# Gated two-layer block, its FP4 MLP on one core: VectorE's roundings, GpSimd's unscalings and the last two pairs in another order

## The reference

```
x = x + tanh(g_xattn[0]) * attention(layernorm(x), ctx, ctx)
x = x + tanh(g_ffn[0])   * experts(layernorm(x))
x = x + tanh(g_xattn[1]) * autocorrelation(layernorm(x), ctx, ctx)
x = x + tanh(g_ffn[1])   * mlp(layernorm(x))
```

```
def fp4_quant_dequant(x):
    scale = max(|x|, over the block) / 6, at least 1e-12
    xn = x / scale
    q = nearest of (0, .5, 1, 1.5, 2, 3, 4, 6) to |xn|, with xn's sign, times scale
gate = fp4_linear(x, w_gate);  y = fp4_linear(x, w_up)      # 128 -> 352
h = silu(gate) * y
return fp4_linear(h, w_down)                                 # 352 -> 128
```

## Time and profile before

| What | Value |
|---|---|
| median of 3 runs | 276.76 us (275.24 to 281.72) |
| span of the profiled execution | 274.8 us |
| own time of the profiled execution | not listed apart from the three runs; the lowest of them is 0.4 us above the span |
| TensorE busy | 253.9 us, 92% |
| VectorE busy | 190.7 us, 69% |
| ScalarE busy | 164.6 us, 60% |
| GpSimd busy | 131.0 us, 48% |
| first hh of the MLP starts | 221.16 us |
| last copy on ScalarE starts | 272.58 us |

### The profile page before, as it was taken

The page is one execution under the profiler, slowest core; times in us unless marked ns, Lnnn a source line. Parts: engine busy times, 40 slices in busy tenths (PEclk is TensorE's granted clock), DMA queues, the critical chain, the costliest instruction groups (busy, mean ns, idle before and its releaser), DMA issues.

```text
span 274.8 us, 6251 instructions
## 1 busy us (share of the span) xinstructions
PE 253.9 (92%) x2152; PEld 196.4 (71%) x2152; DVE 190.7 (69%) x494; ACT 164.6 (60%) x384; POOL 131.0 (48%) x207
## 2 busy tenths in 40 slices
PE   8999999999899989999999999979998784989886
PEld 6655376666577868999999999665785442766675
DVE  3898688888988763253222223885769989999993
ACT  2369985666488654675566667473445793354453
POOL 4566579999402403218992220275066633353230
PEclk9999999999999998999999999999999999799999
DMA  6999000000000209776777771000000000000111
GB/s 191 379 348 403 13 4 2 2 4 0 2 2 4 76 20 377 300 289 265 296 300 291 292 290 63 2 1 1 4 0 0 0 0 2 0 19 23 38 39 38
DMA packets 12191, 30.11 MB, mean 110 GB/s; under 512 B 1024, under 2 KB 5248, under 8 KB 12032
## 3 DMA queue, kind: packets, MB, share of 16 engines
q1 hardware_dynamic: 12160, 29.71, 28.5%
HBM read 9.71 MB, written 1.05 MB: 39 GB/s over the span
## 4 chain that ended last, share of the span: by engine, by line
PE 64%; DVE 20%; issue 7%; ACT 5%; POOL 2%; DVEq 0%; POOLq 0%
PE ps L1403 12%; PE ps L1414 12%; PE ps L1252 6%; DVE s_region L294 4%; PE ps L1226 4%; PE ps L1239 4%; PE ps L1159 3%; DVE s_region L1090 3%; PE ps L1542 3%; PE ps L1150 2%; DVE s_small L1095 2%; PE ps L1262 2%; PE ps L1151 2%; PE ps L1344 2%; DVE s_small L237 2%
## 5 line engine op out<-in xcount | busy, mean ns | idle before, releaser
L631 ACT ACTIVATE s_region<-ps,s_region 128x128 f32<-128x128 f32 x144 | 40.8, 371 | 21.8 <-PE ps L1403 21.8
L960 DVE SCALAR_TENSOR_TENSOR s_ctxT<-ps,s_region,s_ctxT 128x64 f32 x72 | 18.1, 281 | 43.8 <-PE ps L1414 43.8
L1403 PE MATMUL ps<-s_region 128*128 128x128 f32 x288 | 38.0, 276 | 0.3 <-issue 0.3
L1414 PE MATMUL ps<-s_region 128*128 128x128 f32 x288 | 37.9, 275 | 0.0
L1403 PEld LDWEIGHTS ps<-s_region 128*128 128x128 f32 x288 | 34.9, 192 | 0.7 <-issue 0.7
L1414 PEld LDWEIGHTS ps<-s_region 128*128 128x128 f32 x288 | 35.0, 192 | 0.2 <-issue 0.2
L420 POOL COPY s_region<-s_xt 128x64 f32 x72 | 14.8, 234 | 32.3 <-PE ps L1403 24.5
L574 ACT COPY s_region<-ps 128x512 f32<-128x512 f32 x32 | 17.2, 592 | 16.2 <-PE ps L1239 16.2
L830 DVE TENSOR_REDUCE s_small<-ps 128x16 f32<-128x1024 f32 x16 | 19.6, 1224 | 9.7 <-PE ps L1226 9.7
L1599 PE MATMUL ps<-s_region 128*128 128x352 f32 x64 | 21.1, 469 | 5.3 <-DVE s_region L1090 3.7
L301 POOL TENSOR_TENSOR s_region<-s_region,s_small 128x704 f32<-128x704 f32 (+2 forms) x11 | 14.6, 1330 | 22.0 <-DVE s_region L294 21.7
(11 more groups left out here) (230 smaller groups left out, 528.7 us busy)
## 6 DMA issues: line engine op xcount, KB each, us to landing
s_region<-s_wall SPq DMA_DIRECT2D x36, 514.0 KB, 3.0
...
```

What stands on the lines that cost most here:

```text
L631: ins = act.activation(hg[j % 3][:, c, :], ps[:, j % 3, RPT * S * c:RPT * S * (c + 1)], ACT.Gelu, bias=wbuf[j % 6][:, FF + FC * D + c:FF + ...
L960: dve.scalar_tensor_tensor(row, ps[:, 4 + j % 2, S * k:S * k + S], w, row, ALU.mult, ALU.add).then_inc(m["acc_done"], 1)
L1403: ins = mm(ps[:, j % 3, RPT * S * c:RPT * S * (c + 1)], w[:, P * c:P * c + P], xg[j % 4], start=True, stop=True)
L1414: ins = mm(ps[:, 4 + j % 2, 0:RPT * S], w[:, FF + D * c:FF + D * c + D], hg[j % 3][:, c, :], start=(c == 0), stop=(c == FC - 1))
```

## The change

It has five parts, all in the MLP.

- VectorE: in pairs 1 and 3 the roundings of x stand behind the shrink of h, directly ahead of the roundings of h. Ahead of pair 0, `x_scale` and `sum_stats` are split, so that the statistics of group 3 stand between the reciprocal and the shrink of x group 1.
- GpSimd: in q = 1 and 3 it unscales h first and x after it. The small scale operations are gone.
- ScalarE: its copies of turned x and turned h are now activations with the function Copy and the constant scale `FINE / 6` (`unscaled_copy`).
- `WHOLE` is 7: pair 6 is rounded whole, by `h_round(6)` right behind hh of pair 7, and unscaled by GpSimd. Pair 7 alone goes by halves; its shrink is done in halves too, and each half's magnitude waits for its own half.
- TensorE: in q = 3 and 5 the gate product stands ahead of the down products; the turn of an x group stands ahead of `down`, in q = 2 and 4 instead of behind the gate in q = 1 and 3. Before the gate of pair 3 there is a wait for the roundings of x group 2 (`xd_done`). Behind the loop come the turn of pair 6, the residuals of the two halves, the down products of pair 6, both half turns, and the two half products.

SyncE sends seven pairs and two halves instead of six and four.

The diff, without the lists of names and buffers:

```diff
@@ -30,7 +30,7 @@
...
-WHOLE = PAIRS - 2
+WHOLE = PAIRS - 1
...
@@ -285,9 +285,9 @@
...
-        def fp4_scale(eng, amax, sc):
-            return eng.tensor_scalar(sc, amax, FINE / 6.0, None, ALU.mult)
+        def unscaled_copy(act, out, src):
+            return act.activation(out, src, ACT.Copy, scale=FINE / 6.0)
         def fp4_off(eng, out, mag, z):
@@ -466,11 +466,8 @@
...
             def x_unscale(g):
-                pool.wait_ge(m["xv_done"], g + 1)
-                fp4_scale(pool, xmx[g % 2], xsc[g % 2]).then_inc(m["xsc_ready"], 1)
...
-                pool.wait_ge(m["xsc_ready"], g + 1)
-                fp4_unscale(pool, qd[g % 2], xsc[g % 2], 4 * D // BLK, qv[g % 2]).then_inc(m["xq_done"], 1)
+                fp4_unscale(pool, qd[g % 2], xmx[g % 2], 4 * D // BLK, qv[g % 2]).then_inc(m["xq_done"], 1)
...
@@ -485,25 +482,14 @@
...
-            def h_scale(q):
-                pool.wait_ge(m["hv_done"], q + 1)
-                if q >= 3:
-                    pool.wait_ge(m["hq_done"], q - 2)
-                fp4_scale(pool, hmx[q % 3], hsc[q % 3]).then_inc(m["hsc_ready"], 1)
             for q in range(1, WHOLE + 1):
...
+                pool.wait_ge(m["hd_done"], q)
+                if q >= 3:
+                    pool.wait_ge(m["ht_done"], q - 2)
+                fp4_unscale(pool, hd[u], hmx[(q - 1) % 3], 2 * NH, hq[u].rearrange("p a n -> p (a n)")).then_inc(m["hq_done"], 1)
...
-                h_scale(q - 1)
-                pool.wait_ge(m["hd_done"], q)
-                pool.wait_ge(m["hsc_ready"], q)
-                if q >= 3:
-                    pool.wait_ge(m["ht_done"], q - 2)
-                fp4_unscale(pool, hd[u], hsc[(q - 1) % 3], 2 * NH, hq[u].rearrange("p a n -> p (a n)")).then_inc(m["hq_done"], 1)
-            for q in range(WHOLE, PAIRS):
-                h_scale(q)
...
@@ -713,7 +699,7 @@
...
-                act.copy(xqT[g % 2], ps[:, 0, :]).then_inc(m["xqt_used"], 1)
+                unscaled_copy(act, xqT[g % 2], ps[:, 0, :]).then_inc(m["xqt_used"], 1)
             def silu(q):
...
@@ -721,10 +707,10 @@
...
             def magnitude(q):
-                act.wait_ge(m["hv_done"], q + 1)
                 if q >= 2:
...
-                for rows in [slice(0, 2 * NH)] if q < PAIRS - 1 else [slice(0, NH), slice(NH, 2 * NH)]:
+                for n, rows in enumerate([slice(0, 2 * NH)] if q < WHOLE else [slice(0, NH), slice(NH, 2 * NH)]):
+                    act.wait_ge(m["hv_done"], q + 1 + n)
...
             def x_magnitude(g):
@@ -757,7 +743,11 @@
             def half_turned(n):
...
-                act.copy(hT[p % 2][:, t].rearrange("p k b -> p (k b)"), ps[:, 5 + t, 0:MT * P]).then_inc(m["ht_used"], 1)
+                unscaled_copy(act, hT[p % 2][:, t].rearrange("p k b -> p (k b)"), ps[:, 5 + t, 0:MT * P]).then_inc(m["ht_used"], 1)
+            def pair_turned(q):
+                act.wait_ge(m["ht_done"], q + 1)
+                unscaled_copy(act, hT[q % 2].rearrange("p a k b -> p a (k b)"), ps[:, 5:7, 0:MT * P]).then_inc(m["ht_used"], 1)
             def half_finish(n):
...
@@ -768,23 +758,20 @@
...
                 if q >= 3:
...
+                if q >= 2:
+                    pair_turned(q - 2)
...
-                if q >= 2:
-                    act.wait_ge(m["ht_done"], q - 1)
-                    act.copy(hT[q % 2].rearrange("p a k b -> p a (k b)"), ps[:, 5:7, 0:MT * P]).then_inc(m["ht_used"], 1)
...
+            finish(WHOLE - 2)
+            pair_turned(WHOLE - 1)
+            half_turned(0)
...
-            half_turned(0)
...
-            half_turned(2)
...
-            half_turned(3)
-            half_finish(2)
-            half_finish(3)
...
@@ -1059,55 +1046,73 @@
...
+            def sum_spread(g):
...
+            def x_blocks(g):
+                nblk = 4 * D // BLK
+                return xb[:, nblk * g:nblk * (g + 1), :]
             def x_scale(g):
-                u = g % 2
...
-                    dve.wait_ge(m["xsc_ready"], g - 1)
...
-                nblk = 4 * D // BLK
-                src = xb[:, nblk * g:nblk * (g + 1), :]
-                fp4_inverse(dve, dd, src, xmx[u], xin[u])
-                fp4_shrunk(dve, blocks(qv[u]), src[:, :, 0:BLK], spread(xin[u], nblk)).then_inc(m["xv_done"], 1)
+                fp4_inverse(dve, dd, x_blocks(g), xmx[g % 2], xin[g % 2])
+            def x_shrink(g):
+                fp4_shrunk(dve, blocks(qv[g % 2]), x_blocks(g)[:, :, 0:BLK], spread(xin[g % 2], 4 * D // BLK)).then_inc(m["xv_done"], 1)
             def x_round(g):
...
+            def h_round(q):
+                u = q % 2
+                dve.wait_ge(m["hm_done"], q + 1)
+                if q >= 2:
+                    dve.wait_ge(m["hq_done"], q - 1)
+                dd.step(fp4_off(dve, blocks(hd[u]), blocks(hm[u]), hh[u]))
+                fp4_off(dve, hd[u], hm[u], hd[u]).then_inc(m["hd_done"], 1)
             def pair_step(q):
-                u, w, n3 = q % 2, (q - 1) % 2, q % 3
-                if q < PAIRS:
-                    dve.wait_ge(m["sg_done"], q + 1)
-                    dve.wait_ge(m["gu_done"], q + 1)
-                    rows = "p a (n k) -> p a n k"
-                    dve.tensor_tensor(hh[u].rearrange("p (a n) k -> p a n k", a=2), sg[u].rearrange(rows, k=BLK),
-                                      ps[:, 3:5, 0:MLP].rearrange(rows, k=BLK), ALU.mult).then_inc(m["hh_done"], 1)
-                    if q >= 3:
-                        dve.wait_ge(m["hq_done"], q - 2)
-                    dve.wait_ge(m["hh_done"], q + 1)
-                    k = dd.mark(dve.tensor_reduce(hmx[n3], hb[u], AX, ALU.max, apply_absolute_value=True))
-                    if q in (1, 3):
-                        x_round((q + 3) // 2)
-                    if q == 2:
-                        x_scale(3)
-                    dd.after(k)
-                    dd.step(dve.reciprocal(hin[n3], hmx[n3]))
+                u, n3 = q % 2, q % 3
+                dve.wait_ge(m["sg_done"], q + 1)
+                dve.wait_ge(m["gu_done"], q + 1)
+                rows = "p a (n k) -> p a n k"
+                dve.tensor_tensor(hh[u].rearrange("p (a n) k -> p a n k", a=2), sg[u].rearrange(rows, k=BLK),
+                                  ps[:, 3:5, 0:MLP].rearrange(rows, k=BLK), ALU.mult).then_inc(m["hh_done"], 1)
+                if q == WHOLE:
+                    h_round(q - 1)
+                if q >= 3:
+                    dve.wait_ge(m["hq_done"], q - 2)
+                dve.wait_ge(m["hh_done"], q + 1)
+                k = dd.mark(dve.tensor_reduce(hmx[n3], hb[u], AX, ALU.max, apply_absolute_value=True))
+                if q == 2:
+                    x_scale(3)
+                    x_shrink(3)
+                dd.after(k)
+                dd.step(dve.reciprocal(hin[n3], hmx[n3]))
+                if q < WHOLE:
...
-                    if q == 0:
-                        x_scale(2)
-                if 1 <= q <= WHOLE:
-                    dve.wait_ge(m["hm_done"], q)
-                    if q >= 3:
-                        dve.wait_ge(m["hq_done"], q - 2)
-                    dd.step(fp4_off(dve, blocks(hd[w]), blocks(hm[w]), hh[w]))
-                    fp4_off(dve, hd[w], hm[w], hd[w]).then_inc(m["hd_done"], 1)
+                else:
+                    for half in (slice(0, NH), slice(NH, 2 * NH)):
+                        fp4_shrunk(dve, hh[u][:, half], hh[u][:, half], spread(hin[n3][:, half], NH)).then_inc(m["hv_done"], 1)
+                if q == 0:
+                    x_scale(2)
+                    x_shrink(2)
+                if q in (1, 3):
+                    x_round((q + 3) // 2)
+                if 1 <= q < WHOLE:
+                    h_round(q - 1)
             def round_half(n):
@@ -1118,18 +1123,21 @@
...
-                dve.wait_ge(m["hsc_ready"], p + 1)
-                fp4_unscale(dve, hd[u][:, cols], hsc[p % 3][:, NH * t:NH * t + NH], NH, hq[u][:, t, :]).then_inc(m["hq_last"], 1)
+                fp4_unscale(dve, hd[u][:, cols], hmx[p % 3][:, NH * t:NH * t + NH], NH, hq[u][:, t, :]).then_inc(m["hq_last"], 1)
...
+            x_shrink(0)
...
+            sum_spread(2)
...
+            x_shrink(1)
+            sum_spread(3)
...
             for q in range(PAIRS):
...
@@ -1669,25 +1677,24 @@
...
                 if q >= 2:
...
+                if q in (0, 2, 4):
+                    turn_x(q // 2 + 1)
+                if q in (2, 4):
...
-                if q == 0:
-                    turn_x(1)
+                if q == 1:
+                    pe.wait_ge(m["xd_done"], 3)
                 if q + 2 < PAIRS:
...
-                if q in (1, 3):
-                    turn_x((q + 3) // 2)
-            turn_half(0)
+                if q in (3, 5, 6, 7):
+                    down(q - 2)
+            turn_h(WHOLE - 1)
...
+            down(WHOLE - 1)
+            turn_half(0)
...
-            turn_half(2)
-            residual_half(2)
-            residual_half(3)
-            turn_half(3)
-            down_half(2)
-            down_half(3)
...
```

6 lines of the change are left out of this document (3 added, 3 removed).

## The result

| | before | changed |
|---|---|---|
| median of 20 runs, us | 276.27 | 273.24 |
| lowest and highest | 274.62, 281.72 | 272.88, 278.11 |
| span of the profiled execution | 274.8 | 271.3 |

The ratio of the two, from runs side by side on the same chip, is 0.9921 with a 95% interval of 0.9897 to 0.9946: 276.27 times that is 2.2 us faster, between 1.5 and 2.8; the two medians alone differ by 3.0. That ratio leaves out the slow runs, those more than 1.5% above the fastest of their kernel, which by that rule are five of twenty before and two of twenty changed. The forecast was 1.5 us faster, 275.3, and the measured 273.24 lies just inside the range, near its low end.

The account below looks back on a forecast made before the run. VectorE, never idle in the pairs and colliding with GpSimd, was taken to bound the kernel. Terms -0.40 - 1.00 + 0.14 - 0.25 = -1.5 us took 276.76 to 275.3 us, range 273.2 to 277.8.

Parts of the forecast that it names:

- (a): Ahead of pair 0: unscaling starts 0.45 us earlier without GpSimd's small scale, ScalarE's scaled copy costs 0.05; sum -0.40 us.
- (d): Last two pairs: pair 6 rounded whole, its roundings blocked by GpSimd, TensorE's and ScalarE's chain setting the end; -0.25 us.
- (b): Pairs 1 and 3: unscaling of x no longer meets the shrink, -0.62 each, lost gap filling +0.12 each; -1.00 us.
- (c): Pairs 2 and 4: GpSimd's two unscalings in a row clear pair 2 but meet the shrink in pair 4; +0.14 us.
- signs of being wrong: hh of pair 0 to pair 7 not near 38.9; VectorE idle for TensorE in pairs 1-7; clock under 1.00 behind 262 us.
- B: Distance from hh of pair 0 to hh of pair 7, 39.75 us before, forecast near 38.9.
- second rival: Pairs 2 and 4 and tail: collisions move rather than go, gain only 0.5 us, 276.3 us; chance 0.2.
- first rival: Tail: roundings of pair 6 are not blocked by GpSimd, gain 2.0 us, 274.7 us; chance 0.17.
- full price: Tail: roundings of pair 6 fully blocked by GpSimd's unscaling of pair 5, 0.53 us late.
- about 2.9 more: Tail, behind the down products of pair 6: first half turn, its copy and two half products, about 2.9 us.
- (e): TensorE's gates ahead of down products and the wait before the gate of pair 3: worth or costing nothing on the path.
- third rival: Tail: TensorE's clock falls, five pieces lose 0.5 us each, 2.5 us in all, 277.8 us; chance 0.08.

Follow-up runs that it names:

- e4: Changed kernel with the small scale of x back on GpSimd for all four groups and a plain ScalarE copy of turned x; 276.78 us.
- e12: Changed kernel with the small scale on GpSimd back for x groups 0 and 1 alone, which lie ahead of the pairs; 275.48 us.
- e1: Changed kernel with x roundings of pairs 1 and 3 back between reduction and reciprocal, and GpSimd unscaling x ahead of h; 277.84 us.
- e3: Changed kernel with the last two pairs by halves again (six whole pairs) in all engines; 278.45 us.
- e5: Changed kernel with the roundings of pair 6 behind the reduction of pair 7 instead of behind its hh; 273.32 us.
- e2: Changed kernel with only GpSimd's order back (x unscaled ahead of h in pairs 1 and 3), VectorE's order as changed; 275.99 us.
- e8: Changed kernel with each gate product behind the down products again (q = 3 and 5); 273.02 us.
- e9: Changed kernel without TensorE's wait ahead of the gate of pair 3; 278.05 us.
- e10: e5 with TensorE also turning the first half of pair 7 ahead of the down products of pair 6; 275.96 us.

## Why the prediction was right, point by point

The direction and the mechanism held; (a) and (d) each came out about 0.15 us larger than priced, (b) as priced, and the leftover collision (c) 0.11 smaller. None of the signs of being wrong came: B is near 38.9, VectorE waits for TensorE in none of pairs 1 to 7, and the clock behind 262 us stays at 1.00.

(a) Ahead of pair 0, forecast -0.40, measured -0.56, shown by e4 and e12 (10.75 and 10.76 with the scale back). The step that was mis-sized is the price of the scale: I took 0.45 from the scale's start to the unscaling's. But the scale itself had started 0.28 after the operation ahead of it; now the unscaling starts 0.15 after the same operation. The distance between the neighbours was 0.73 and is 0.15: 0.58. Of that the slower copy gives back 0.02 (0.58 to 0.60), not 0.05. That VectorE was ready is as forecast (it stands idle for 0.81 us ahead of hh of pair 0), but what the split statistics are worth no run tests; with the scale back they gave nothing.

Here the Trainium skill (ScalarE: Activation LUTs, What ACT_TABLE_LOAD costs) was nearer than the 0.05 that I took: by its 93 ns for an operand from memory about 0.01 of the 0.105 us would be left for the constant scale, an estimate, and the trace shows 0.02.

(b) Pairs 1 and 3, forecast -1.00. Pair 1 went from 6.72 to 6.21 and pair 3 from 6.80 to 6.28: -1.03. e1 gives it back.

(c) Pair 4, forecast +0.14, measured +0.03 (4.95 to 4.98). I let GpSimd's two unscalings take 2.53 with a gap of 0.08 between them; they took 2.43. By the rule of the earlier trace rows that leaves 0.03, as measured. That the second rival was near is shown by e4: GpSimd ends 0.56 us later, and the shrink of pair 4 loses 0.57 and that of x group 3 in pair 2 0.12. It did not come about in the changed kernel because another part of the change took away the scale that would stand between the two unscalings.

(d) The tail, forecast -0.25, measured -0.40, given back by e3. The blocked roundings are the step on which the forecast and the first rival parted. They were blocked in full: 2.45 against 1.81 is 0.64, where I had 0.53. The difference is only in their start, which I put 0.08 too late; what follows them starts at 3.16 after hh, and I had 3.14. The rival is ruled out by this row and by e5, where they take 1.81 with GpSimd done. Here the rule of the Trainium skill (SBUF — State Buffer, SBUF: two separate sides), an exclusive lock for VectorE operations with two SBUF inputs against GpSimd operations that read SBUF, agrees with the trace for shrinks, roundings and unscalings, in both directions (e2).

One pair of rows does not fit it. In the changed kernel GpSimd's power operation on 4 columns starts 0.12 us ahead of the roundings of x group 1, and nobody loses:

```profile
216.64 1.04 POOL L269 TENSOR_TENSOR s_small<-s_small,s_par 128x4 f32<-128x4 f32 x1
...
216.76 1.42 DVE L294 SCALAR_TENSOR_TENSOR s_region<-s_region 128x512 f32<-128x512 f32 x2 [0.20 <-ACT s_region L720]
```

With the roundings first it is GpSimd alone that loses (1.43). So the full price that I took holds for the wide unscalings, and the row of the power operation could not tell it either way. What sets the two kinds apart no run here shows.

Which chain sets the end I had right, but not by how much. TensorE's and ScalarE's ran as forecast up to the half turns: GpSimd unscales pair 6 from 3.32 on (forecast 3.3), ScalarE's copy starts at 6.25 (6.2), the down products end at 8.56 (8.5). The mis-sized term is the last one, the "about 2.9 more" from there to the last copy: it took 2.71 (269.03 - 266.32), where the two half turns stand in one row of 0.98 us. So the end is at 11.27 and not 11.4. VectorE's chain would end at 11.08, where I had 11.0, and the two are nearly tied.

(e) The gates were costed at nothing; e8 shows 0.17 us. I looked at TensorE's slack for the up products, which was right, and not at what stands behind the delayed copy in ScalarE's list. The wait ahead of the gate of pair 3 was costed at nothing, and e9 shows that.

The third rival, a low clock in the tail, did not come about in the changed kernel. e4 shows that it can, at a price of at most 0.59, where I had 2.5. The pieces that were slow there are those of pair 5, 1.6 us in all on TensorE; the five pieces of pair 6 and the halves, which I had priced, ran at their usual speed. I had named no condition for it but TensorE's waiting, and e10 (1.33 us, clock 1.00) shows that this is not enough of one. What decides it stays open.

The time itself, 273.24, is 2.1 us under the forecast of 275.3, and only 0.43 of that is the change coming out larger than priced. Another 0.49 is the start of the sum: three runs put the median of before at 276.76, twenty put it at 276.27. The rest, some 1.1 us, is that the two medians differ by 3.03 where the pieces differ by 1.94: 11 of the 20 times of the changed kernel lie within 0.4 us of its lowest, and 4 of the 20 of before do, and the lowest times of the two differ by 1.74. Why the changed kernel's runs lie closer to their lowest is open. So it is in part luck that 273.24 fell inside the range, by 0.04 us: its lower end was made for a rival that the runs rule out. I had also written that a measurement of this kernel can hardly tell a change under 2%; twenty runs of each told one of 0.8%.

What goes with the difference between runs is seen ahead of the change. The granted clock of one stretch, then the reduction of x group 0, in three executions (the changed kernel, before, and e3):

```profile
95.00:110.00 15.00, 13.84 (x111) 11.86 (x111) 8.54 (x37) 8.95 (x23) 3.57 (x18) 1.00 0.54 215
```

```profile
95.00:110.00 15.00, 13.98 (x100) 11.51 (x99) 8.06 (x35) 7.90 (x20) 3.40 (x17) 0.89 0.53 209
```

```profile
95.00:110.00 15.00, 13.99 (x84) 11.35 (x83) 7.68 (x35) 6.22 (x12) 2.77 (x14) 0.75 0.53 210
```

With a clock of 1.00 the reduction starts at 208.79, with 0.89 at 210.40, with 0.75 (and 0.93 in the 20 us after) at 213.73. All three kernels run the same instructions up to there. Of the twelve profiled executions three had 1.00 (MLP from 208.5 to 208.8 us), and the other nine began it 1.4 to 5.2 us later. Why the clock differs there from run to run no run shows.
